# Two layers of cross attention: mixed tiles of maxima 64 columns at a time, and loads spread out

## The reference

```python
q = hidden_state @ Wq + bq
k = encoder_hidden_state @ Wk + bk
v = encoder_hidden_state @ Wv + bv
scores = jnp.einsum('bkgld,bksd->bkgls', q, k) * scale
scores = scores + encoder_attention_mask[:, :, None, :, :]
attn = jax.nn.softmax(scores, axis=-1)
out = jnp.einsum('bkgls,bksd->bkgld', attn, v)
out = out.transpose(0, 3, 1, 2, 4).reshape(b, l, H) @ Wo + bo
x = out + hidden_state
return (x - mu) * jax.lax.rsqrt(var + EPS) * gamma + beta
```

## Time and profile before

| | |
|---|---|
| median of 3 runs | 1738.77 us (1736.56 to 1738.89) |
| the profiled execution | 1738.81 us |
| its span, first to last instruction | 1737.0 us |
| TensorE / VectorE / ScalarE / GpSimd busy | 98% / 73% / 60% / 33% of the span |
| TensorE's matmuls | 10881, of them 2560 for maxima |
| maxima's matmuls, 128 and 32 columns | 377.5 and 65.6 us busy |
| VectorE idle until maxima's matmuls | 392.5 us in 308 waits |

### The profile page before, as it was taken

One profiled execution on the slowest core, in us unless ns is written; L12 is line 12 of the kernel. 1 busy time (PEld: TensorE's weight loads), 2 busy tenths in 40 slices (PEclk: granted clock), 3 DMA queues, 4 the chain that ended last, 5 costly groups with the idle time before them and its releaser, 6 DMA issues. The chain is left out here.

```text
span 1737.0 us, 35992 instructions
## 1 busy us (share of the span) xinstructions
PE 1695.1 (98%) x10881; PEld 1005.9 (58%) x10881; DVE 1267.2 (73%) x1713; ACT 1042.3 (60%) x2370; POOL 572.3 (33%) x1169
## 2 busy tenths in 40 slices
PE   5999999999999999999999999999999999999997
PEld 3555566665565665565665565655665655656652
DVE  5567777787777777777777776777767877767776
ACT  2556666666665656665656665666656666656564
POOL 3133332333332333332333323333323333323332
PEclk8899999999999999999999999999999999999999
DMA  8546555455545465555565454455454455453541
GB/s 283 146 121 170 147 122 143 128 145 143 147 120 142 124 151 145 135 130 147 128 156 145 114 136 130 118 135 145 105 135 125 128 138 139 109 135 115 139 113 55
DMA packets 288390, 235.83 MB, mean 136 GB/s; under 512 B 140858, under 2 KB 262964, under 8 KB 288084
## 3 DMA queue, kind: packets, MB, share of 16 engines
q1 hardware_dynamic: 266852, 204.14, 43.8%
q10 hardware_dynamic: 21488, 31.06, 7.3%
HBM read 101.39 MB, written 22.02 MB: 71 GB/s over the span
## 5 line engine op out<-in xcount | busy, mean ns | idle before, releaser
L922 DVE TENSOR_REDUCE mx<-ms 128x2 f32<-128x750 f32 x896 | 809.2, 924 | 399.0 <-PE ms L1090 392.5
L740 ACT ACTIVATE probs<-sc 125x448 f32<-125x448 f32 x1522 | 744.6, 542 | 281.8 <-PE sc L1061 274.7
L1090 PE MATMUL ms<-ks,qs 96*128 96x375 bf16 (+1 forms) x2560 | 443.0, 327 | 11.4 <-DVE mx L922 8.7
L1061 PE MATMUL sc<-qs,ks 99*125 99x448 bf16 x1522 | 429.2, 358 | 6.0 <-DMA qs<-mT 3.7
L1111 PE MATMUL pv<-probs,vs 125*32 125x448 f32 x3048 | 313.2, 544 | 0.0
L1061 PEld LDWEIGHTS sc<-qs,ks 99*125 99x125 bf16 x1522 | 192.7, 137 | 204.2 <-ACT probs L740 127.8
L1090 PEld LDWEIGHTS ms<-ks,qs 96*128 96x128 bf16 (+1 forms) x2560 | 174.8, 98 | 194.3 <-issue 66.2
L1165 PE MATMUL job<-wo,on 128*112 128x512 f32 x504 | 258.2, 594 | 0.0
L936 DVE RECIPROCAL orec<-osum 128x112 f32<-128x112 f32 x256 | 213.0, 834 | 6.8 <-DMA osum<-oraw 6.8
L1183 PE MATMUL job<-xT,wq 128*128 128x224 f32 x1008 | 214.5, 356 | 0.0
L1134 PEld LDWEIGHTS job<-wv,ctxT 128*125 128x125 f32 x1536 | 191.5, 189 | 16.5 <-issue 0.3
(11 more groups left out here) (70 smaller groups left out, 1034.5 us busy)
## 6 DMA issues: line engine op xcount, KB each, us to landing
ctxT<-in_ctxT SPq DMA_DIRECT2D x64, 750.0 KB, 4.7
qs<-qp SPq DMA_DIRECT2D x756, 56.0 KB, 2.5
ks<-kp SPq DMA_DIRECT2D x765, 46.9 KB, 2.7
osum<-oraw ACTq DMA_DIRECT2D x125, 112.0 KB, 2.9
oc<-oraw ACTq DMA_DIRECT2D x125, 112.0 KB, 3.6
mask<-in_mask SPq DMA_DIRECT2D x64, 164.1 KB, 5.1
xT<-in_xT SPq DMA_DIRECT2D x32, 224.0 KB, 4.6
xin<-in_x SPq DMA_DIRECT2D x32, 224.0 KB, 3.0
```

What stands on the lines that cost most here:

```text
L740: nc.scalar.activation(probs[0:KCS, k, j, :], bank[0:KCS, 0:GL], ACT.Exp)\
L922: nc.vector.tensor_reduce(mx[o][:, cols], ms[n % 2][:, :, 0:S2], AX_X, ALU.max).then_inc(max_done[o], 1)
L1061: last = nc.tensor.matmul(bank[0:KCS, 0:GL], ks[p][0:KM, g, rows], qs[p][0:KM, g, :], start=True, stop=not masked)
L1090: last = nc.tensor.matmul(to, qs[o][0:KT, group, cols], ks[o][0:KT, group, :], start=True, stop=not masked)
```

## The change

Five edits. COL becomes 64, so a mixed tile takes two matmuls and a mixed pair four. In the opening the second context and Wv are loaded behind all seven pieces of bits (all from SyncE now) and behind copies, ScalarE's share of the copies of keys goes to SyncE, memsets on GpSimd move behind the identities, and TensorE runs 3 and 8 extra matmuls (`keep_clock`). The slot (1, -1) is run once: the second unit's keys (k = 0 to 3) and the first unit's values (k = 8 to 10) stand between its maxima, after a wait for Wv at its start. Slot (0, 0) has a table row of its own, with maxima from k = 2 on. Weights are issued over eight slots, with a second pair of semaphores `rows_in`.

```diff
@@ tables @@
-BEARLY = 2
-COL = 32
+COL = 64
+CLOCK = (3, 8)
-KEYS_AT = [{2: (0,), 3: (1, 2), 4: (3,)}, {2: (0, 1), 3: (2, 3)}, {0: (0, 1, 2, 3)}]
-VALUES_AT = [{1: (0, 1), 2: (2,)}, {4: (0,), 5: (1,), 6: (2,)}, {0: (0, 1, 2)}]
+KEYS_AT = [{2: (0,), 3: (1, 2), 4: (3,)}, {2: (0, 1), 3: (2, 3)}, {0: (0,), 1: (1,), 2: (2,), 3: (3,)}]
+VALUES_AT = [{1: (0, 1), 2: (2,)}, {4: (0,), 5: (1,), 6: (2,)}, {8: (0,), 9: (1,), 10: (2,)}]
-QUERY_PARTS_AT = [7, 5, 1]
-QUERY_REST_AT = [9, 6, 2]
-SEND_QUERIES_AT = 3
+QUERY_PARTS_AT = [7, 5, 0]
+QUERY_REST_AT = [9, 6, 1]
+SEND_QUERIES_AT = (4, 7)
+for table in (STEPS_AT, KEYS_AT, VALUES_AT, COLUMNS_AT, MIXED_AT, QUERY_PARTS_AT, QUERY_REST_AT, WORK_FIRST, WORK_LAST):
+    table.append(table[0])
+STEPS_AT[3] = [0, 0, 2, 2, 1, 2, 1, 1, 0, 2, 0, 1]
+MIXED_AT[3] = (2, 8)
+KEYS_AT[3] = {3: (0,), 4: (1, 2), 5: (3,)}
...
-    return 2 if first_values(p, i) else p
+    return 2 if first_values(p, i) else 3 if isinstance(i, int) and (p, i) == (0, 0) else p
...
+def first_rows(p, i):
+    return isinstance(i, int) and (p, i) == (0, 1)
@@ SyncE @@
             def opening_slot(p):
+                if p == 1:
+                    max_rows(0, 0, 1)
                 sp.wait_ge(k_p3[p], 1)
                 if p == 0:
                     stack_terms(0, 0, ks[0], kp[0], 1)
+                    stack_terms(0, 1, ks[0], kp[0], 1, of=(1, 2))
                     sp.wait_ge(q_p1[0], 2)
                     stack_terms(0, 0, qs[0], qp, 0, of=(0,))
-                    stack_terms(0, 1, ks[0], kp[0], 1, of=(1, 2))
+                    stack_terms(0, 1, ks[0], kp[0], 1, of=(0,))
+                    load_ctx(1, 0, 0)
+                    load_wv(0, w_v)
                     stack_terms(0, 1, qs[0], qp, 0, of=(0,))
                     load_mask(0, 0, 0)
                 else:
@@
-                    max_rows(0, 0, 1)
-                    load_wo(0, w_in[0])
-                    load_rows(0, w_in[0])
+                    load_wo(0, w_in[0], slice(0, 2))
@@
-            def next_layer(p, i):
+            def weights(p, i):
                 if (p, i) == (0, 0):
+                    load_wo(0, w_in[0], slice(2, NG))
+                    load_row(bo, 0, "bo", w_in[0])
+                if (p, i) == (1, 0):
+                    load_row(gamma, 0, "gamma", rows_in[0])
+                    load_row(beta, 0, "beta", rows_in[0])
+                if (p, i) == (0, 1):
                     load_wk(1, w_in[1])
                     load_wv(1, w_in[1])
-                    load_rows(1, w_in[1])
-                if (p, i) == (1, 0):
+                if (p, i) == (1, 1):
                     load_wq(1, w_in[1], slice(0, 2))
-                if (p, i) == (0, 1):
+                if (p, i) == (0, PER - 2):
                     load_wq(1, w_in[1], slice(2, DC))
-                if (p, i) == (1, 1):
-                    load_wo(1, w_in[1], slice(0, 2))
-                if (p, i) == (0, PER - 2):
-                    load_wo(1, w_in[1], slice(2, NG))
+                if (p, i) == (1, PER - 2):
+                    load_wo(1, rows_in[1], slice(0, 2))
+                if (p, i) == (0, PER - 1):
+                    load_wo(1, rows_in[1], slice(2, NG))
+                if (p, i) == (1, PER - 1):
+                    for dst, key in ((bo, "bo"), (gamma, "gamma"), (beta, "beta")):
+                        load_row(dst, 1, key, rows_in[1])
...
-            load_ctx(1, 0, 0)
-            load_wv(0, w_v)
-            for n in range(BEARLY, BLOADS):
+            for n in range(BLOADS):
@@ VectorE @@
-                if first_outputs(p, i):
-                    dve.wait_ge(w_in[0], 16 * NW[0])
+                if first_rows(p, i):
+                    dve.wait_ge(rows_in[0], 16 * NR[0])
@@ TensorE @@
+                    if first_values(p, i):
+                        pe.wait_ge(w_v, 16 * NV)
...
-            for p in range(PAR):
-                slots(False, opening=True)(p, -1, exists(p, -1), layers(p, -1))
+            keep_clock(CLOCK[0])
+            pe.wait_ge(w_k, 16 * NK)
+            slots(False)(*FIRST, exists(*FIRST), layers(*FIRST))
+            keep_clock(CLOCK[1])
```

More of the change, by code:

```diff
@@ L101, in step_order @@
             for _ in range(count):
-                half, tiles = (0 if k == 0 else 1, (MIXED, MIXED + TILES // 2)) if part == 1 else \
+                half, tiles = (MIXED_AT[q].index(k), (MIXED, MIXED + TILES // 2)) if part == 1 else \
                     (whole // len(WHOLE), WHOLE[whole % len(WHOLE)])
@@ L109, in step_order @@
     return order
-ORDER = [step_order(q) for q in range(PAR + 1)]
+ORDER = [step_order(q) for q in range(len(STEPS_AT))]
 OPENS = [[min(n for at in o for n, h, _, _ in at if h == half) for half in range(2)] for o in ORDER]
@@ L156, in first_outputs @@
 def first_outputs(p, i):
[L158 removed]
+    return isinstance(i, int) and (p, i) in ((1, 0), (1, PER))
+def first_rows(p, i):
+    return isinstance(i, int) and (p, i) == (0, 1)
 def last_scores(p, i):
@@ L289, in cross_attention_two_layers @@
         w_in = two(sem, "w_in")
+        rows_in = two(sem, "rows_in")
         mf_in = [sem(f"mf_in{n}") for n in range(BLOADS)]
@@ L504, in slot @@
                 if isinstance(i, int):
-                    next_layer(p, i)
+                    weights(p, i)
                 if isinstance(i, int) and (p, i) == (1, PER):
@@ L650, in residual_rows @@
                 def residual_rows():
+                    if first_outputs(p, i) and i == 0:
+                        pool.wait_ge(w_in[0], 16 * NW[0])
+                    if first_outputs(p, i) and i == PER:
+                        pool.wait_ge(rows_in[1], 16 * NR[1])
                     pool.wait_ge(x_in[o], 16 * (post + 1))
@@ L871, in slot @@
                             cast_rests(h)
-                    if opens(p, i) and k == SEND_QUERIES_AT:
+                    if opens(p, i) and k == SEND_QUERIES_AT[0]:
                         act.wait_ge(q_p1[p], 2)
+                        send(0, qs[p], qp, 0, (0,))
+                    if opens(p, i) and k == SEND_QUERIES_AT[1]:
                         act.wait_ge(q_p2[p], 2)
                         act.wait_ge(q_p3[p], 2)
-                        send(0, qs[p], qp, 0, range(PARTS))
-            for n in range(BEARLY):
-                act.dma_start(mbits[:, BROW * n:BROW * (n + 1)], mbits_d[n]).then_inc(mf_in[n], 16)
+                        send(0, qs[p], qp, 0, (1, 2))
             act.wait_ge(warm_set, 1)
@@ L1022, in _, with slots @@
         def _(pe):
-            def slots(masked, opening=False):
+            def slots(masked):
                 def slot(p, i, has, lay):
@@ L1037, in slot @@
                     job_free = [(o_evac[p], stored + 1) if s_ok else (mt_evac[p], 2 * main + 1) if m_ok else None]
-                    if first_values(p, i):
-                        job_free[0] = (q_evac, NG // 2) if opening else (v_ready[o], 1)
+                    if isinstance(i, int) and (p, i) == (0, 0):
+                        job_free[0] = (v_ready[p], 1)
                     def take_job_bank():
@@ L1217, in maxima @@
                         def maxima(part):
-                            for n, half, tiles, place in ORDER[q][k] if a_ok and not opening else ():
+                            for n, half, tiles, place in ORDER[q][k] if a_ok else ():
                                 if place == part:
                                     maximum(n, half, tiles, place)
-                        if k == 0 and a_ok and masked and not opening:
+                        if k == 0 and a_ok and masked:
                             pe.wait_ge(mask_in[o], 16 * (ahead + 1))
-                        if k == PIECES - 1 and a_ok and not masked and not opening:
+                        if k == PIECES - 1 and a_ok and not masked:
                             pe.wait_ge(mask_in[o], 16 * (ahead + 1))
@@ L1246, in slot @@
                             maxima(1)
-                        if k == COLUMNS_AT[q][0] and a_ok and not opening:
+                        if k == COLUMNS_AT[q][0] and a_ok:
                             max_columns(o, 0, ahead)
@@ L1254, in _, with keep_clock @@
             pe.wait_ge(idd, 3)
+            def keep_clock(times):
+                for _ in range(times):
+                    nc.tensor.matmul(ms[0][0:S, 0, 0:GL], ident4[:, 0, :], ident4[:, :, :].rearrange("p c l -> p (c l)"),
+                                     start=True, stop=True)
+            keep_clock(CLOCK[0])
             pe.wait_ge(w_k, 16 * NK)
-            for p in range(PAR):
-                slots(False, opening=True)(p, -1, exists(p, -1), layers(p, -1))
-            pe.wait_ge(idd, 3)
+            slots(False)(*FIRST, exists(*FIRST), layers(*FIRST))
+            keep_clock(CLOCK[1])
             pe.wait_ge(flag_col, BLOADS + 1)
```

50 lines of the change are left out of this document (23 added, 27 removed).

## The result

The changed kernel takes 1756.62 us, median of 4 runs (1755.17 to 1760.06), against 1738.83 (1736.56 to 1739.17) of the kernel before, run beside it. The ratio is 1.0107, 95% interval 1.0092 to 1.0121: slower by 17.8 us where +10.6 was forecast. The direction was right and the size too small: the median lies at the very top of the range of 1735 to 1757, and the ratio times the median of before, 1757.4, just above it.

The account below looks back on a forecast made before the run. TensorE, busy for 98% of the span, was taken to bound the kernel. The terms +11.9 + 4.9 - 2.8 - 6.0 + 2.1 + 0.5 summed to +10.6 us, giving 1749.4 us, with a range of 1735 to 1757.

Parts of the forecast that it names:

- (a): Mixed steps behind the weighted values: 64 columns add a border from 32, 0.095 us net at 125 steps, +11.9 us.
- (d): Slot (0, 0): entered from dense work, it may start at full clock; -2.8 us (-3.5 to +1).
- (f): Start of slot (0, 1): VectorE waits for gamma and beta, then TensorE for VectorE; +2.1 us (0 to 4).
- (e): Weights spread over eight slots: the 3.73 us stall at 92.50 and the half clock after it go; -6.0 us.
- the opening: Stretch up to the first scores: start of the maxima unchanged at 33.6, slot (1, -1) longer; +4.9 us.
- the layer's border: Where layers meet: six half or full loads spread over four slots; +0.5 us (0 to +1.5).
- The rival of no loss: Mixed steps: no loss between 32 and 64 columns, (a) is -1.6, time 1735.9 us; chance 0.13.
- that of twos one by one: Mixed steps: twos don't run together or are treated as 128 wide, 40 us more, 1789 us; chance 0.05.
- (b): Opening, bits loaded ahead of the second context: same bytes must land, first maxima unchanged at 33.6; 0 us.
- (c): Slot (1, -1): second unit's keys and the values within the first maxima at half clock, 18.1 against 13.2; +4.9 us.
- a rival with a chance of 0.06: Slot (0, 1): the wait of (f) is longer and TensorE loses its clock after it; 4.6 more, 1754 us; chance 0.06.

Follow-up runs that it names:

- the late wait: The changed kernel with VectorE's wait for gamma and beta moved from the start of slot (0, 1) to their first use (k = 4): 1751.83 us, 1.0072.
- The last run: The kernel before with spread loads, VectorE's gamma and beta wait at first use, and extra matmuls holding TensorE's clock up to slot (0, 0): 1735.53 us, 0.9973.

## Why the prediction was right or wrong, point by point

Direction, places and mechanisms came as put; what failed are sizes. The forecast is 7.2 us short: 3.1 in the price of a mixed step (a), 1.9 in slot (0, 0) (d), 1.7 in the half clock behind the new wait (f), 0.4 in (e) and 0.1 in the opening, less 1.2 at the layer's border; 1.1 stays open.

Lengths of slots below are from first scores to first scores in the two timelines, before and after.

**(a) 64 columns, forecast +11.9: right in mechanism, too small.** The rival of no loss (1736) and that of twos one by one (1789) both fell. The term that was mis-sized is the net price of a mixed step: 0.095 us, made of a border of 0.108 less 0.013 saved on issue, and 0.108 at most. Measured is 0.119: 0.113 behind the values and 0.006 more in the step. Times 125 that is 15.0 us with the step's price rounded to 0.12, and the two runs with COL changed alone gave 14.7 and 14.6. The step that failed most is the saving. With two matmuls in a group and not four, what follows does start 0.02 us sooner after the second group (0.26 for 0.28), but the second group starts 0.02 us later after the first (0.18 for 0.16), so nothing is left of it; that is 0.019 of the 0.024 us missed. The border itself was nearly right, but by a guess: 0.09 from the other borders, and 0.02 for weights, a term that no row showed. The trace of before holds a border out of the four-wide fp32 values, in the last slots, where scores of 125 columns follow them and not a mixed step:

```profile
1713.37 2.46 PE L1111 MATMUL pv<-probs,vs 125*32 125x448 f32 x24
1715.76 0.59 PE L1061 MATMUL ms<-qs,ks 99*125 99x448 bf16 x2
```

From values to scores it takes 2.39 us, not 2.28: 0.11, the price that was then paid 125 times. It could have been read before the run.

By the Trainium skill's rule ("TensorEngine Tiling (Array Packing)", "Key Properties") the border between 32 and 64 had to be paid, and the runs agree: 0.11 us here.

**(b) and (c) The opening, forecast +4.9: right, +5.0 at the first scores.** (b) came as put, with a wait for bv of 6.24 us and maxima at 33.98 for 33.6, but its reason did not hold: it is not that the same bytes must have landed. With the old order of loads and the new program the maxima start at 41.55. The order counts, by the landings above through the copies that compete with whatever bits are left. (c) forecast 18.1 us for the slot and 17.81 came, by the mechanism put (half clock, 0.65 over the first 8 us), which the run with TensorE kept at work confirms. How near the sum came owes something to the execution: in the three other profiles with this opening and these loads (COL = 32, the late wait, and both) the first scores stand at 53.80, 53.48 and 55.78, not at 51.79, though each of those executions was 2.0 to 3.8 us above its kernel's median.

**(d) Slot (0, 0), forecast -2.8: -0.9** (28.05 to 27.19). The clock was full from the start as hoped. What took its place are VectorE's maxima, which now begin two pieces later and all fall into the rest of the slot: TensorE waits 0.44 us for an exponential and 0.80 for maxima at 59.08 where before it waited for neither, and one mixed border is in it. I had priced the clock and not the later start. The last run bears this out: with the old table and full clock the slot took 25.00 us, 2.9 less than 27.91, so the clock was priced rightly; with the new table, full clock and COL = 32 it took 27.06 in each of the four profiles. So the new table, and what came into the slot with the new opening, cost the 2 us between.

**(e) The spread loads, forecast -6.0: -5.55**, with 0.24 of borders in it (31.77 to 26.22). The stall of 3.73 us went to 0.36; a wait of 1.10 for copies of the queries behind it is new.

**(f) The new wait, forecast +2.1: +3.8**, (0, 1) from 27.70 to 31.72 less 0.24. Place, cause and wait were right (4.92 us for VectorE, 1.98 for TensorE, against 2.1 forecast). Mis-sized was what follows: 1.8 us of the half clock after it, which I had only as a rival with a chance of 0.06, at 4.6 us.

**The layer's border, forecast +0.5: about -0.7.** From the scores of slot (0, 14) to those of (0, 19), ten slots, it took 263.80 us before and 265.45 after: 1.65 more, where ten slots of borders alone would be 2.4.

**Not in the forecast: slot (0, 31)**, 22.05 us before and 25.41 after. In this slot TensorE waits for VectorE in both kernels, until 1697.00 before (1.05 us) and until 1712.66 after (1.06). During that wait the clock fell to half in the profile after (granted 0.50 from 1712.10 to 1718.80) and stayed full in that before (1.00 from 1697.00 to 1703.00). The wait, of 1.02 to 1.06 us, stands in all 14 profiles: the slot is 22.0 to 22.3 us long in the three where the clock stayed full, 23.8 to 24.4 in nine, and 25.3 and 25.4 in the changed kernel with COL = 32 and 64. So its 3.4 us of the 18.3 by which the two profiled executions differ are chance, but for 0.24 of borders. Without it, 15.0 for the borders, 5.0 - 0.9 - 5.5 + 3.8 for opening and loads and -0.7 at the layer's border make 16.7; the medians differ by 17.8, and the 1.1 us between are not accounted for.

## What to carry to other kernels

Before matmuls are made wider or fewer, look at what stands beside them on TensorE: here 32 columns behind 32 cost nothing extra, and each border between widths of 32, 64 and full tiles costs 0.09 to 0.11 us, as much as 0.6 to 0.7 of a bf16 matmul of 375 columns (0.16). Scores of 125 columns and maxima of 128 side by side pay nothing (0.38 and 0.32 us for two of each). Look through the whole trace for the border that the change will make; it may stand at a rare place, as here in the last slots. Where a shared load is split up, move each wait to the first use of what it brings; here one wait set at the head of a slot for rows needed four pieces later gave back all that the spread loads gained. And a short wait on a full TensorE is to be priced with the half clock that may follow it.

## What the hardware showed that was not expected

- The border out of fp32 values of 32 columns costs 0.11 us, into 64, 125 and 128 columns alike (2.39 or 2.40 us from values to what follows, for 2.28); those into values and out of bf16 tiles 0.09.
- After waits of 1 to 2 us TensorE's clock sometimes fell to half for 3 to 7 us and sometimes did not, at the same place of nearly the same programs (slot (0, 31), after a wait of 1.02 to 1.06 us: 22.0 to 25.4 us over the profiles).
- Loads of 750 KB came every 1.8 to 1.9 us before the copies began to land and every 3.6 us beside copies of some 50 KB, at first with full engines (share 1.11, 199 GB/s), then with a mean share of 0.46. The cause stays open.
- The moment at which the last small load of the opening landed varied between executions of nearly the same program by 3 us (first maxima at 33.98, 35.48, 35.73 and 36.82).
